# Attention block on one core: half of the rounding of x moved from ScalarE to VectorE, with a new hand-written order on every engine

## The reference

```python
theta = x @ W_theta                      # 1024 x 32
phi   = maxpool2x2(x @ W_phi)            # 256 x 32
g     = maxpool2x2(x @ W_g)              # 256 x 128
beta  = softmax(theta @ phi.T, axis=-1)  # 1024 x 256
out   = gamma * ((beta @ g) @ W_o) + x
```

## Time and profile before

| What | Value |
|---|---|
| Time, median of 3 runs (lowest to highest) | 232.94 us (232.38 to 233.38) |
| The profiled execution's own time | 232.19 us |
| Its span in the trace | 230.40 us |
| TensorE busy | 217.5 us (94%) |
| ScalarE busy | 200.7 us (87%) |
| VectorE busy | 181.8 us (79%) |
| GpSimd busy | 157.7 us (68%) |
| Granted TensorE clock, mean | 0.998 |
| DMA: moved, mean busy share of the 16 DMA engines in queue q1 | 57.02 MB, 70.5% |

### The profile page before, as it was taken

The page is one execution under the profiler, slowest core; times in us unless marked ns, Lnnn a source line. Parts: engine busy times, 40 slices in busy tenths (PEclk is TensorE's granted clock), DMA queues, the critical chain, the costliest instruction groups (busy, mean ns, idle before and its releaser), DMA issues.

```text
span 230.4 us, 4086 instructions
## 1 busy us (share of the span) xinstructions
PE 217.5 (94%) x1144; PEld 158.8 (69%) x1144; DVE 181.8 (79%) x380; ACT 200.7 (87%) x536; POOL 157.7 (68%) x106
## 2 busy tenths in 40 slices
PE   7697989999999999999999999999999999989992
PEld 5245776677858676786867678686767678666781
DVE  4589759587878879787878978787897978986674
ACT  3599999998989989898989989898998989998750
POOL 1297848996977679686767869676777967616350
PEclk9999999999999999999999999999999999999999
DMA  6992563489895868888696877868588764066954
GB/s 207 395 383 70 144 255 136 133 284 319 278 335 160 318 238 267 292 283 315 189 351 220 284 304 235 311 211 323 215 289 306 224 221 173 39 196 265 306 242 182
DMA packets 19638, 57.02 MB, mean 247 GB/s; under 512 B 3424, under 2 KB 4640, under 8 KB 19616
## 3 DMA queue, kind: packets, MB, share of 16 engines
q1 hardware_dynamic: 19472, 56.64, 70.5%
q10 hardware_dynamic: 144, 0.13, 0.2%
HBM read 33.88 MB, written 16.78 MB: 220 GB/s over the span
## 4 chain that ended last, share of the span: by engine, by line
PE 82%; ACT 7%; DMA 5%; DVE 2%; issue 2%; SPq 1%; DVEq 0%; ACTq 0%
PE mixed L383 13%; PE value L300 12%; PE proj L272 11%; PE out L417 9%; PE score L343 8%; PE mixed L387 6%; PE shift L367 6%; PE value L309 5%; PE proj L417 4%; PE value L417 4%; DMA x_t<-in_xt 3%; ACT score L626 3%; DVE y_sb L935 2%; DMA out<-y_sb 2%; PE mixed L324 1%
## 5 line engine op out<-in xcount | busy, mean ns | idle before, releaser
L782 POOL TENSOR_TENSOR x_lo<-x_t,x_hi 128x1024 fp32r<-128x1024 f32 x30 | 71.8, 2396 | 35.5 <-ACT x_hi L566 35.4
L787 POOL TENSOR_TENSOR e_lo<-e_sb,e_hi 128x512 fp32r<-128x512 f32 x64 | 81.1, 1288 | 18.1 <-ACT e_sb L638 16.8
L626 ACT ACTIVATE score<-score,neg_parts 128x256 f32<-128x256 f32 x128 | 57.5, 455 | 1.4 <-DVE neg_parts L907 0.8
L907 DVE TENSOR_REDUCE neg_parts<-score 128x2 f32<-128x512 f32 x64 | 42.1, 679 | 7.1 <-PE score L343 6.8
L635 ACT ACTIVATE e_hi<-shift 128x512 fp32r<-128x512 f32 x64 | 39.8, 621 | 0.2
L638 ACT ACTIVATE e_sb<-shift 128x512 f32<-128x512 f32 x64 | 39.9, 623 | 0.0
L566 ACT CAST x_hi<-x_t 128x1024 fp32r<-128x1024 f32 x31 | 32.8, 1060 | 3.2 <-DMA x_t<-in_xt 3.2
L919 DVE TENSOR_TENSOR tmp_lo<-mixed,tmp_hi 128x512 fp32r<-128x512 f32 x31 | 21.4, 691 | 16.0 <-ACT tmp_hi L644 16.0
L272 PE MATMUL proj<-x_t,w_sb 128*64 128x512 f32 x120 | 29.1, 604 | 1.2 <-DMA x_t<-in_xt 1.2
L343 PEld LDWEIGHTS score<-phi,theta 96*128 96x128 f32 x128 | 18.9, 189 | 15.6 <-ACT score L626 13.0
L935 DVE SCALAR_TENSOR_TENSOR y_sb<-out,r_sum,x_n 128x256 f32<-128x256 f32 x62 | 27.8, 475 | 1.5 <-PE proj L417 1.5
(11 more groups left out here) (103 smaller groups left out, 429.3 us busy)
## 6 DMA issues: line engine op xcount, KB each, us to landing
x_t<-in_xt SPq DMA_DIRECT2D x32, 512.0 KB, 5.8
x_n<-in_xn SPq DMA_DIRECT2D x32, 512.0 KB, 6.2
out<-y_sb SPq DMA_DIRECT2D x31, 512.0 KB, 3.8
theta<-theta_hi SPq DMA_DIRECT2D x56, 64.0 KB, 3.3
theta<-theta_lo SPq DMA_DIRECT2D x28, 64.0 KB, 2.0
phi<-phi SPq DMA_DIRECT2D x14, 32.0 KB, 2.1
theta<-neg_hi SPq DMA_DIRECT2D x16, 4.0 KB
theta<-neg_lo SPq DMA_DIRECT2D x16, 4.0 KB
```

The lines of the kernel that those rows point to most:

```text
L626: last = nc.scalar.activation(score[n % 2][:, NK * k:NK * (k + 1)], score[n % 2][:, NK * k:NK * (k + 1)], ACT.Exp, bias=neg_parts[:, t:t + ...
L782: nc.gpsimd.tensor_tensor(x_lo[:, i % 2, h], x_t[:, i % 3, h], x_hi[:, i % 2, h].bitcast(f32), ALU.subtract).then_inc(x_lo_ready, 1)
L787: nc.gpsimd.tensor_tensor(e_lo[:, i % 2, n, :], e_sb[:, n, :], e_hi[:, i % 2, n, :].bitcast(f32), ALU.subtract).then_inc(e_lo_ready, 1)
L907: v.tensor_reduce(neg_parts[:, 2 * n:2 * n + 2], score[n % 2][:, :].rearrange("p (t k) -> p t k", t=2), AX.X, ALU.max, negate=True).then_i ...
```

## The change

For h = 1, images 1 to 15 are rounded by a new function on VectorE, `x_high_one`. The counting semaphore becomes one for each half. The reciprocals on VectorE wait for the finishes of two images before. The order is new on all five instruction streams; the loop of ten passes is now written `for s in range(6, 16)` and holds nearly the same work, cut at another place. The number of instructions of each kind is otherwise unchanged. Cut to its core:

```diff
-        x_hi_ready, x_lo_ready = sem("x_hi_ready"), sem("x_lo_ready")
+        x_hi_ready = [sem(f"x_hi_ready{h}") for h in range(2)]
+        x_lo_ready = sem("x_lo_ready")
...
-                pe.wait_ge(x_hi_ready, 2 * i + h)
+                pe.wait_ge(x_hi_ready[h], i + h)
...
-                pool.wait_ge(x_hi_ready, 2 * i + h)
+                pool.wait_ge(x_hi_ready[h], i + h)
...
+            def x_high_one(i):
+                dve.wait_ge(xt_in[i % 3][1], loads_t(i, 1))
+                if i >= 2:
+                    dve.wait_ge(g_ready, 2 * (i - 2) + 2)
+                dve.wait_ge(x_hi_ready[1], i)
+                v.tensor_copy(x_hi[:, i % 2, 1], x_t[:, i % 3, 1]).then_inc(x_hi_ready[1], 1)
...
             def reciprocals(i):
                 dve.wait_ge(sum_ready, 4 * i + 4)
+                if i >= 2:
+                    dve.wait_ge(y_ready, TILES * (i - 2) + TILES)
```

The new loop of each engine, SP first:

```diff
+            for s in range(6, 16):
+                phi_and_lo_into_stack(s - 2)
+                load_n(s - 3, 0)
                 load_n(s - 3, 1)
+                load_t(s, 0)
                 store(s - 4, 0)
+                load_t(s, 1)
+                store(s - 4, 1)
                 theta_hi_into_stack(s - 1)
                 max_into_stack(s - 2)
```

TensorE:

```diff
+            for s in range(6, 16):
+                values(s - 1, 0)
+                turn_max(s - 2)
+                mix(s - 3, 0)
+                values(s - 1, 1)
+                mix(s - 3, 1)
+                outputs(s - 3, 0)
+                shifted(s - 2, 0)
+                shifted(s - 2, 1)
+                outputs(s - 3, 1)
+                turn_g(s - 1)
+                outputs(s - 3, 2)
+                scores(s - 1, 0)
+                shifted(s - 2, 2)
                 shifted(s - 2, 3)
+                scores(s - 1, 1)
+                outputs(s - 3, 3)
                 theta_phi(s)
                 scores(s - 1, 2)
                 scores(s - 1, 3)
```

ScalarE:

```diff
+            for s in range(6, 16):
+                sums(s - 2, 0)
+                sums(s - 2, 1)
+                theta_high(s - 1)
+                exps(s - 3, 3)
+                neg_high(s - 2)
+                x_high(s, 0)
+                tmp_high(s - 3, 0)
+                phi_high(s - 1)
+                sums(s - 2, 2)
+                sums(s - 2, 3)
+                tmp_high(s - 3, 1)
+                exps(s - 2, 0)
+                exps(s - 2, 1)
+                g_high(s - 1)
+                exps(s - 2, 2)
```

GpSimd, its start and its loop:

```diff
             theta_copy(0)
             x_low(1, 0)
-            x_low(1, 1)
             pool.wait_ge(wo_in, 16)
             nc.gpsimd.tensor_scalar(w_og[:, :], wo_sb[:, 0:C], wo_sb[:, C:C + 1], None, ALU.mult).then_inc(wog_ready, 1)
+            x_low(1, 1)
             x_low(2, 0)
...
+            for s in range(6, 16):
+                e_low(s - 3, 3)
+                e_low(s - 2, 0)
+                e_low(s - 2, 1)
+                x_low(s, 0)
+                x_low(s, 1)
                 e_low(s - 2, 2)
```

VectorE, its start and its loop:

```diff
+            phi_pool(1)
             maxima(0, 0)
             maxima(0, 1)
-            phi_pool(1)
             theta_low(1)
+            x_high_one(1)
             maxima(0, 2)
+            g_pool(0, 1)
             maxima(0, 3)
...
+            phi_low(1)
+            neg_low(0)
+            x_high_one(2)
+            phi_pool(2)
+            maxima(1, 0)
...
+            for s in range(6, 16):
+                phi_pool(s - 1)
+                neg_low(s - 2)
+                g_pool(s - 1, 0)
+                theta_low(s - 1)
+                tmp_low(s - 3, 0)
+                x_high_one(s)
+                phi_low(s - 1)
+                g_pool(s - 1, 1)
+                tmp_low(s - 3, 1)
+                finishes(s - 3, (0, 1, 2, 3, 4, 5))
+                maxima(s - 1, 0)
+                maxima(s - 1, 1)
+                finish(s - 3, 6)
+                reciprocals(s - 2)
+                finish(s - 3, 7)
                 g_low(s - 1)
                 maxima(s - 1, 2)
                 maxima(s - 1, 3)
```

More of the change, by code:

```diff
@@ L200, in _ @@
             phi_and_lo_into_stack(1)
+            load_n(0, 0)
+            load_t(3, 1)
             max_into_stack(0)
@@ L483, in _ @@
             scores(3, 2)
+            shifted(2, 3)
             scores(3, 3)
@@ L504, in _ @@
                 scores(s - 1, 3)
-                values(s, 0)
-                turn_max(s - 1)
-                mix(s - 2, 0)
-                values(s, 1)
-                mix(s - 2, 1)
-                outputs(s - 2, 0)
-                shifted(s - 1, 0)
-                outputs(s - 2, 1)
-                turn_g(s)
-                shifted(s - 1, 1)
-                outputs(s - 2, 2)
-                shifted(s - 1, 2)
-                outputs(s - 2, 3)
-                scores(s, 0)
-                scores(s, 1)
-            theta_phi(LAST)
-            scores(LAST - 1, 2)
-            shifted(LAST - 2, 3)
-            scores(LAST - 1, 3)
             values(LAST, 0)
@@ L565, in x_high @@
                     act.wait_ge(g_ready, 2 * (i - 2) + h + 1)
-                nc.scalar.copy(x_hi[:, i % 2, h], x_t[:, i % 3, h]).then_inc(x_hi_ready, 1)
+                nc.scalar.copy(x_hi[:, i % 2, h], x_t[:, i % 3, h]).then_inc(x_hi_ready[h], 1)
             def first_x_high(c):
@@ L760, in _ @@
             sums(LAST, 2)
+            sums(LAST, 3)
             tmp_high(LAST - 1, 1)
@@ L1013, in _ @@
             finishes(1, (6, 7))
-            g_low(3)
+            reciprocals(2)
             maxima(3, 2)
             maxima(3, 3)
+            g_low(3)
+            theta_low(4)
+            g_pool(4, 0)
             phi_pool(4)
-            reciprocals(2)
             neg_low(3)
-            g_pool(4, 0)
             tmp_low(2, 0)
-            theta_low(4)
+            g_pool(4, 1)
             phi_low(4)
-            g_pool(4, 1)
+            x_high_one(5)
+            reciprocals(3)
             tmp_low(2, 1)
-            finishes(2, (0, 1, 2, 3, 4))
@@ L1027, in _ @@
-            reciprocals(3)
-            finish(2, 5)
+            finishes(2, (0, 1, 2, 3, 4, 5))
             maxima(4, 0)
             maxima(4, 1)
-            finish(2, 6)
-            for s in range(5, 15):
+            finishes(2, (6, 7))
+            g_low(4)
+            maxima(4, 2)
+            maxima(4, 3)
+            for s in range(6, 16):
[14 more added lines that the diff above has]
+                finish(s - 3, 7)
@@ L1033, in _ @@
                 g_low(s - 1)
-                finish(s - 3, 7)
                 maxima(s - 1, 2)
                 maxima(s - 1, 3)
-                neg_low(s - 1)
-                g_pool(s, 0)
-                phi_pool(s)
-                tmp_low(s - 2, 0)
-                theta_low(s)
-                phi_low(s)
-                g_pool(s, 1)
-                tmp_low(s - 2, 1)
-                finishes(s - 2, (0, 1, 2, 3, 4, 5))
-                maxima(s, 0)
-                reciprocals(s - 1)
```

253 lines of the change are left out of this document (105 added, 148 removed).

## The result

The change makes the kernel slower: 238.88 us median (237.99 to 239.72, 4 runs) against 233.16 (232.38 to 233.94) for the kernel before beside it, ratio 1.0253 with a 95% interval of 1.0223 to 1.0283. The profiled execution took 238.61 us, 1.8 of it outside the span.

A forecast was written before the change was run, and what follows sets the result against it. TensorE was taken to bound the loop. Start +0.3, ten passes +2.6 and end -0.8 summed to +2.1 us: 234.3 on the profiled execution, 235.0 on the median's scale; range 226.5 to 237.5.

The forecast's parts named there:

- The pass if the copy waits: Loop: the copy sits behind an e_low for about 0.8 us; pass 13.49 against 13.23 us, +0.26 each.
- The ring: Loop: outputs, shifted, e_hi, e_sb, GpSimd's block of six, waiting copy, phi_low, next outputs; sum 13.49 us a pass.
- to spare: Loop: phi_low ends at 5.7 us, mix(s-3, 1) at 6.1, so a copy wait up to 0.4 us is harmless.
- The rule of the Trainium skill: A two-port VectorE copy and any GpSimd instruction exclude each other; whichever issues second is blocked until the first is over.
- So 12.90 us if VectorE takes the copy freely: Loop: TensorE's 0.36 us wait for ScalarE goes, 13.23 to 12.87; turn_max about 0.03 us late.
- the first rival: No contention: the copy runs beside GpSimd at its own speed; -5.8 us, 227.1 us; chance 0.20.
- The start: +0.3: First images: x_high_one(2) waits for x_low(2, 0), first exponential about 25.5 against 25.28 us; +0.3 us.
- Cover enough, but thinner than before: Loop's x_t loads: second load issued 7.4 us before its copy, median landing 5.8, so 1.6 us left; no cost.
- the third rival: Later x_t loads or maxima's DMAs arrive too late: 0.3 us a pass on top, 238 us; chance 0.05.
- The end: -0.8: Last images: GpSimd's last four e_low start 17.75 instead of 18.53 us after values(15, 0); -0.8 us.
- No contention: Copy runs beside GpSimd at its own speed: ten passes of 12.90 us, -5.8 us, 227.1 us; chance 0.20.
- GpSimd pays: Copy goes through, the e_low beside it is stretched by up to 0.65 us; -2.8, 230.1 us; chance 0.17.

The follow-up runs named there:

- e2_later: Changed kernel with the loop's x_high_one(s) moved behind phi_low(s-1) and g_pool(s-1, 1): 237.62 us, ratio 1.0228.
- e8_old_gap: Kernel before, semaphore per half, only the loop's ten second-half copies on VectorE, ahead of neg_low(s - 1): 232.78 us, ratio 0.9977.
- e15: Kernel before, copies on ScalarE, with only TensorE's scores(s, 0) moved ahead of outputs(s - 2, 3): 231.6 us, ratio 0.9961.
- e5_start: Changed kernel with x_high_one(2) moved right behind x_high_one(1) and x_high_one(5) behind tmp_low(2, 1), loop untouched: 236.16 us, ratio 1.0153.
- e3_loads: Changed kernel with load_t(s, 1) issued ahead of store(s-4, 0) in SP's loop: 238.66 us, ratio 1.0233.
- e6_all: Changed kernel with the edits of e2_later, e3_loads and e5_start together: 233.29 us, ratio 0.9995.
- e14_copy_first: e13_sums_scores with the copy moved ahead of both maxima(s - 1, 2) and (s - 1, 3): 231.9 us, ratio 0.9973.
- e13_sums_scores: e8_old_gap with sums(s - 1, 3) ahead of tmp_high(s - 2, 1) and scores(s, 0) ahead of outputs(s - 2, 3): 253.77 us, ratio 1.0922.
- e1_reduce: Changed kernel with all 15 VectorE copies made a max-reduction over an axis of one element: 237.17 us, ratio 1.019.
- e7_old_order: Kernel before, semaphore per half, only the loop's ten second-half copies on VectorE, behind phi_low(s): 235.53 us, ratio 1.0127.

## Why the prediction was right and wrong

The direction and the mechanism came as forecast: the copy waits for GpSimd, and it is the wait that stops TensorE. The size did not: 235.0 forecast, 238.88 measured, above the range. The sum was +2.1 us on the span; 6.4 came. The step that failed most is the start, +0.3 in the sum and +2.75 measured; behind it come the late loads.

**The pass if the copy waits: right.** 13.49 forecast, 13.46 measured, in six of ten passes. The ring is there in the trace, piece by piece: GpSimd's block 9.74 us (9.78 forecast), from its end to the outputs 1.34 (1.42), from there to the next block 2.38 (2.29). The copy stood behind a GpSimd instruction until it ended, and phi_low, tmp_low and the outputs came late behind it. The duration of the copy alone was right as well (0.71 forecast, 0.67). Two sizes inside were not. The wait was put at 0.8 us; asked at 127.08, with e_low over at 127.59, it was 0.51, and the record 1.06 where 1.4 was forecast. And of the 0.4 us "to spare" only some 0.12 was there, an estimate: the outputs at 128.93, 0.39 earlier, would be at 128.54, and TensorE would be free for them at 128.66 (6.04 us behind values at 122.62, the distance in e2_later, 121.91 to 127.95). The two ways in which the prediction prices a wait do not agree either: 12.90 + 0.8 - 0.4 is 13.3, the ring gives 13.49, and it was the ring that held. The rule of the Trainium skill that the prediction weighed ("SBUF — State Buffer", "Who interferes with whom") agrees, with the copies of 2.40, 2.44 and 2.91 us where VectorE asked second, and with GpSimd's 1.21 for 0.93 (e2_later) and 2.76 for 2.40 (e8_old_gap) where GpSimd did.

**"So 12.90 us if VectorE takes the copy freely": wrong.** 13.12 measured (e2_later), and 13.11 in the old order with the copy on ScalarE (e15). The step that failed reads "since TensorE waited for ScalarE 0.36 us a pass, that wait should go". First, its size: what went was 0.83 - 0.58 = 0.25. The 0.81 us of the earlier trace rows are no stall of TensorE at all; in after, where the first score follows theta_phi 1.87 us after its start just as before, the weight load shows the same 0.81. Second, removing it shortened a pass by only 0.11. Third, it was not ScalarE's load that made it: with the copy off ScalarE it stayed (0.83 us from the scores at 131.42 to the values at 132.25), because the freed 1.05 us lay ahead of a wait for the mixing (e8_old_gap), and with the copy still on ScalarE it went once TensorE took scores(s, 0) one place earlier (e15_scores_act). This error made the forecast's lower tail and the first rival (227.1) look likely; it was not in the +0.26 a pass.

**"The start: +0.3": wrong, +2.75.** The sum had walked only the first exponential. Image 5 was never walked: `x_high_one(5)` stands ahead of `tmp_low(2, 1)` and behind 1.88 us of an x_lo, +1.23, of which moving the copy took back 0.94 (e5_start). The rest, +1.5 by theta_phi(4) and +2.24 by theta_phi(3), is the copy of image 2 asked 0.6 later than walked (20.47 for 19.85), the stand of 2.09 us behind it, and TensorE's fall to 1.2 GHz, which the sum did not have. In e3_loads the first images kept 1.00, and theta_phi(3) was at +0.23, which the forecast came near to, with a copy of 1.83 us and a stand of 1.53. Between it and after lie 2.01 us at theta_phi(3): 0.27 were there at theta_phi(2), 0.56 is the longer stand, and 1.18 came behind it, with the lower clock. That these 1.18 are the clock's is read from two profiles, not from a run made for it; in the last images a fall cost 1.2 to 1.4 us (below). Why the clock fell is open.

**"Cover enough, but thinner than before": wrong in three passes.** +1.6 us in the profiled execution; the third rival had it at 0.3 us in every pass, with a chance of 0.05. What came was 0.34, 0.62 and 0.66 in some passes. A median of 5.8 us to landing says nothing of the load that takes 9; the cover of 1.6 us had to be held against the longest.

**"The end: -0.8": right in sign, -0.25.**

Together: 2.45 of the missing 4.3 us are the start, 1.6 minus 0.3 the passes, 0.5 the end.

**The rivals.** No contention is refuted by the copies of 2.4 us. GpSimd pays did happen where the copy was asked first: in e8_old_gap, 0.18 us ahead, and in e2_later, where the copy at 16.12 was 0.27 ahead of w_og (1.21 us for 0.93). It happened in after too (w_og 1.45 for 0.93), where w_og's record begins 0.06 us ahead, so at such distances the starts of the records do not say who came first.

## What to carry to other kernels

Before moving work off an engine because another waits for it, look what stands in front of the awaited result: here a wait for a third engine, and the freed microsecond fell into it. Where two engines exclude each other, what counts is who asks first; a placement that wins by 0.18 us is a trap for the next edit, and one where it lost in one kernel and won in another with the same first images (e5_start, e6_all) is no better. Put such an instruction well away from the other engine's: the copy in e14_copy_first was 1.86 us ahead (119.70 against 121.56) and none waited. Walk every copy that the change adds, those in the unrolled first images too: one misplaced copy there cost as much as five passes of the loop.

## What the runs showed beyond that

- Who asked first was worth 21.9 us of the whole, a lower mean clock included (0.964 against 0.995 in the profiles): e13_sums_scores (253.77) and e14_copy_first (231.9) differ in nothing but the copy's place on VectorE, two maxima apart, and in the former the copy's record begins 0.02 us behind GpSimd's.
- A VectorE reduction of 1024 elements over an axis of one took 1.20 to 1.22 us in all 15 places, beside any work of GpSimd, where the copy took 0.67 to 2.44. A VectorE subtraction of 512 elements with both inputs in SBUF had held GpSimd up before.
- A matmul of 512 columns in the stretch at 0.50 took 0.78 us (at 27.33), where the same one took 0.40 at 28.61. In the last images a fall to 0.50, some 3.4 us long, cost 1.2 to 1.4 us: from theta_phi(15) to the end of the span it took 35.86, 35.85 and 36.00 us in e2_later, e3_loads and e6_all, where it fell, and 34.63, 34.55 and 34.54 in after, e1_reduce and e5_start, where it did not, with the same order there.
- The length of the stand ahead of it does not say whether the clock falls. In the first images it fell behind stands of 2.09 (after), 2.18 (e2_later) and 2.75 us (e5_start) and not behind 1.53 (e3_loads); but with the first images of the kernel before it fell in e7_old_order and e15_scores_act behind the same stand of 1.31 and 1.30 us behind which the kernel before kept 1.00. There it cost 0.33 and 0.24 us from theta_phi(2) to theta_phi(3). In the last images all six kernels had stood 0.96 and 0.50 us. The kernel before, then e7_old_order:

```profile
24.00:26.00 2.00, 1.96 (x10) 1.32 (x8) 1.91 (x6) 2.00 (x9) 1.31 (x1) 1.00 0.28 70
```

```profile
24.00:26.00 2.00, 2.00 (x6) 1.61 (x5) 1.85 (x5) 2.00 (x10) 1.50 (x1) 0.50 0.28 70
```
